# Reordering TensorE's work in the expert and feed-forward stage of a fused attention block

## The reference, cut to what matters

```python
x = x + attn(cond(x, ...))                     # x: 64 x 64 x 1024, float32
x = x + ffn(cond2(x, ...))

def cond2(x, ids, W, Wr, A, B):                # linear layer with gated LoRA experts
    base = einsum('btd,od->bto', x, W)
    logits = einsum('btd,ed->bte', x, Wr) + one_hot(ids) * 5.0
    topw, topi = top_k(logits, 2)
    gates = sum(one_hot(topi) * softmax(topw))
    h = einsum('btd,erd->bter', x, A)
    return base + 2.0 * einsum('bter,bte,eor->bto', h, gates, B)

def ffn(z):                                    # z in bfloat16, quantized to whole numbers per row
    qg, sg = dynamic_quant(z, inv_gate); qu, su = dynamic_quant(z, inv_up)
    inter = silu(quant_gemm(qg, sg, w_gate)) * quant_gemm(qu, su, w_up)
    qi, si = dynamic_quant(clip(inter, -10, 10), inv_inter)
    return quant_gemm(qi, si, w_down)
```

## Time and profile before

| what | value |
|---|---|
| time, median of 3 runs | 2393.21 us (2391.35 to 2397.13) |
| the profiled execution | 2398.05 us, its span 2396.1 us |
| TensorE busy | 2268.3 us (95% of the span) |
| TensorE weight loads busy | 1836.1 us (77%) |
| VectorE busy | 1307.3 us (55%) |
| ScalarE busy | 701.5 us (29%) |
| GpSimd busy | 1319.8 us (55%) |
| granted TensorE clock, mean | 0.982 |

### The profile page before, as it was taken

How to read it: one execution, slowest core, us unless ns; L and a number is a source line. 1 busy time by engine, 2 the same in 40 slices (tenths; PEclk the granted TensorE clock), 3 DMA queues, 4 the chain that set the end, 5 groups by cost and what they waited for, 6 DMA issues and landing times. The chain is left out here.

```text
span 2396.1 us, 48171 instructions
## 1 busy us (share of the span) xinstructions
PE 2268.3 (95%) x19520; PEld 1836.1 (77%) x19552; DVE 1307.3 (55%) x2248; ACT 701.5 (29%) x1122; POOL 1319.8 (55%) x1091
## 2 busy tenths in 40 slices
PE   6999999999999999999996999998999999999996
PEld 5888877888778888788885888886777777777774
DVE  5354464445644555545455322224677777777775
ACT  3222242222422223322223101012343333333332
POOL 6887878887778786888750000001455445445443
PEclk9999999999999999999998999998999999999998
DMA  4211122111221112121116844444011111111111
GB/s 139 65 60 57 61 98 68 63 59 63 80 89 56 66 54 72 65 69 54 63 37 202 239 165 132 132 166 132 19 53 53 39 49 53 47 41 53 53 35 44
DMA packets 130374, 188.33 MB, mean 79 GB/s; under 512 B 16162, under 2 KB 61346, under 8 KB 130210
## 3 DMA queue, kind: packets, MB, share of 16 engines
q1 hardware_dynamic: 118130, 165.92, 21.7%
q10 hardware_dynamic: 9216, 16.78, 1.8%
q0 software_dynamic: 2864, 3.28, 0.8%
HBM read 138.76 MB, written 50.33 MB: 79 GB/s over the span
## 5 line engine op out<-in xcount | busy, mean ns | idle before, releaser
L662 PE MATMUL acc<-y_hi,w_slot_hi 128*128 128x512 f32 x1344 | 541.6, 403 | 29.8 <-DVE unit L521 9.0
L662 PE MATMUL acc<-y_hi,w_slot_lo 128*128 128x512 f32 x1344 | 528.6, 393 | 0.0
L662 PE MATMUL acc<-y_lo,w_slot_hi 128*128 128x512 f32 x1344 | 527.7, 393 | 0.0
L313 POOL TENSOR_TENSOR w_slot_lo<-w_raw,w_slot_hi 128x512 fp32r<-128x512 f32 x329 | 424.3, 1290 | 26.3
L662 PEld LDWEIGHTS acc<-y_hi,w_slot_hi 128*128 128x128 f32 x1344 | 254.7, 189 | 90.2 <-issue 27.3
L311 POOL CAST w_slot_hi<-w_raw 128x512 fp32r<-128x512 f32 x329 | 218.0, 663 | 169.2 <-PE acc L662 134.8
L662 PEld LDWEIGHTS acc<-y_hi,w_slot_lo 128*128 128x128 f32 x1344 | 254.6, 189 | 54.8
L662 PEld LDWEIGHTS acc<-y_lo,w_slot_hi 128*128 128x128 f32 x1344 | 255.1, 190 | 48.9
L316 POOL TENSOR_TENSOR w_raw<-w_raw 128x512 f32<-128x512 f32 x188 | 259.4, 1380 | 25.6 <-DMA w_raw<-wu 20.5
L1094 POOL TENSOR_TENSOR raw<-raw,c_raw 128x1024 f32<-128x1024 f32 x32 | 76.2, 2380 | 347.0 <-DVE raw L1277 347.0
L1291 PE MATMUL z_ps<-w_hi,x_hi 128*128 128x512 f32 x512 | 219.1, 428 | 1.4 <-DVE w_lo L1150 1.2
(11 more groups left out here) (166 smaller groups left out, 3840.1 us busy)
## 6 DMA issues: line engine op xcount, KB each, us to landing
w_raw<-wu SPq DMA_DIRECT2D x192, 256.0 KB, 3.1
c_raw<-context_T SPq DMA_DIRECT2D x9, 2048.0 KB, 11.0
c_raw<-x_T SPq DMA_DIRECT2D x33, 512.0 KB, 4.6
x_c<-xT SPq DMA_DIRECT2D x64, 256.0 KB, 3.5
x_T<-out_c ACTq DMA_DIRECT2D x64, 256.0 KB, 3.7
out<-raw SPq DMA_DIRECT2D x32, 512.0 KB, 3.1
context_T<-cx SPq DMA_DIRECT2D x63, 256.0 KB, 3.5
x_raw<-x SPq DMA_DIRECT2D x27, 512.0 KB, 4.7
```

Source lines behind the costliest of these rows:

```text
L313: pool.tensor_tensor(w_lo[:, k], raw, w_hi[:, k].bitcast(F32), ALU.subtract).then_inc(w_set, 1)
L662: ins = pe.matmul(bank, w[:, k, c, :], v[:, k, c, :], start=(k in (0, 1, 5) and c == 0 and i == 0), stop=(c == C // 2 - 1 and i == 2), ski ...
```

## The change

In TensorE's body of this stage the order changes in four places. The transposes of the inner rows stand behind `linear` chunks 4 and 5, together with the scales' row; the down product stands behind `linear` chunks 6 and 7; the LoRA product follows it; gate and up stand last, one directly behind the other. In VectorE's body `zb` times inv_gate (`xg_set`) is ahead of `gt`. No instruction is added or removed, and the waits move with their instructions.

```diff
--- before.py
+++ after.py
@@ -1179,11 +1179,6 @@
 
         def body(t, j, has):
             two, three = (j + 2) % 4, (j + 1) % 4
-            if has(3):
-                dve.wait_ge(gu_mm, t * 2 - 5)
-                dve.wait_ge(p1_set, t - 3)
-                dve.scalar_tensor_tensor(gt[:], g_ps[:, 0], sc[:, three, 0:1], sg_all[:], ALU.mult, ALU.mult)\
-                    .then_inc(gt_set, 1)
             if has(2):
                 if isinstance(t, int) and t == 2:
                     dve.wait_ge(inv_in, 32)
@@ -1191,6 +1186,10 @@
                 dve.wait_ge(qb_set, t * 2 - 4)
                 dve.tensor_tensor(xs[0], zb[:], ig_all, ALU.mult).then_inc(xg_set, 1)
             if has(3):
+                dve.wait_ge(gu_mm, t * 2 - 5)
+                dve.wait_ge(p1_set, t - 3)
+                dve.scalar_tensor_tensor(gt[:], g_ps[:, 0], sc[:, three, 0:1], sg_all[:], ALU.mult, ALU.mult)\
+                    .then_inc(gt_set, 1)
                 dve.wait_ge(gu_mm, t * 2 - 4)
                 dve.wait_ge(p2_set, t - 3)
                 dve.scalar_tensor_tensor(ut[:], g_ps[:, 1], sc[:, three, 1:2], su_all[:], ALU.mult, ALU.mult)\
@@ -1325,21 +1324,23 @@
                 elif t > 1:
                     pe.wait_ge(hl_set, t - 1)
                 pe.transpose(ht_ps, hg[:], ident[:]).then_inc(ht_mm, 1)
+            if has(1):
+                linear(one, 1, range(4, 6), first)
             if has(3):
                 pe.wait_ge(ut_set, t - 2)
                 pe.wait_ge(qi_set, t - 2)
                 for c in range(CI):
                     ins = pe.transpose(qi_ps[:, c], qi[:, c * P:(c + 1) * P], ident_b[:])
                 ins.then_inc(ti_mm, 1)
-            if has(1):
-                linear(one, 1, range(4, 6), first)
-            if has(3):
                 pe.wait_ge(diag_set, t - 2)
                 if has(1):
                     pe.wait_ge(hl_set, t)
                 else:
                     pe.wait_ge(si_set, t - 3)
                 pe.matmul(si_ps, ones[:], diag[:], start=True, stop=True).then_inc(si_mm, 1)
+            if has(1):
+                linear(one, 1, range(6, 8), first)
+            if has(3):
                 if isinstance(t, int) and t == 3:
                     pe.wait_ge(dn_in, 16)
                 pe.wait_ge(qiT_set, t - 2)
@@ -1348,19 +1349,6 @@
                         ins = pe.matmul(g_ps[:, f // 4, (f % 4) * P:(f % 4 + 1) * P],
                                         dn_w[:, c, f * P:(f + 1) * P], qiT[:, c], start=(c == 0), stop=(c == CI - 1))
                 ins.then_inc(d_mm, 1)
-            if has(1):
-                linear(one, 1, range(6, 8), first)
-
-            def gate_up(i):
-                pe.wait_ge(qT_set, t * 2 - 3 + i)
-                for c in range(C):
-                    ins = pe.matmul(g_ps[:, i], qT[i][:, c], gu_w[:, c, i], start=(c == 0), stop=(c == C - 1))
-                ins.then_inc(gu_mm, 1)
-
-            if has(2):
-                if has(3):
-                    pe.wait_ge(o1_set, t - 2)
-                gate_up(0)
             if has(1):
                 if first:
                     pe.wait_ge(b_lo_set, 1)
@@ -1371,7 +1359,13 @@
                                         start=False, stop=(k == 2))
                     ins.then_inc(z_mm, 1)
             if has(2):
-                gate_up(1)
+                if has(3):
+                    pe.wait_ge(o1_set, t - 2)
+                for i in range(2):
+                    pe.wait_ge(qT_set, t * 2 - 3 + i)
+                    for c in range(C):
+                        ins = pe.matmul(g_ps[:, i], qT[i][:, c], gu_w[:, c, i], start=(c == 0), stop=(c == C - 1))
+                    ins.then_inc(gu_mm, 1)
 
         tile_loop(pe, body)
```

## The result

The changed kernel takes 2449.49 us (median of 4 runs, 2447.80 to 2453.02), the kernel before beside it 2394.64 us: the ratio is 1.0236, 95% interval [1.0215, 1.0257]. The forecast was slower, 2453 us. The profiled execution took 2449.45 us with a span of 2447.5 us; TensorE is busy for 2269.7 us, as before, which is now 93% of the span, and the granted clock is 0.982 of full speed, as before.

What follows compares the result with a forecast made beforehand. A loop through every engine and the load of x was taken as the bound: 1.11 + 1.0 = 2.1 us a tile, 58.8 us over 28 tiles, +1.1 for the first, total +59.9, giving 2453 us; range 2421 to 2464.

Steps and rivals of the forecast that it cites:

- The pace is set by the loop through the load of x: Expert and feed-forward stage: a 22.33 us loop through every engine and the load of x sets the pace, not TensorE's work.
- The down product behind one more piece: TensorE, last q transpose to end of down product: one more 1.48 us linear piece there, 23.44 against 22.33 us, +1.11.
- The meeting of zb x inv_gate with the last sum: VectorE's zb x inv_gate starts just ahead of GpSimd's sum with x (L1094) and holds it: +1.0 us a tile.
- The exchange at qi: TensorE: putting the qi transposes behind linear 4:6 removes the wait for qi, a gain of 0.38 us.
- The LoRA product: TensorE: LoRA product directly behind the down product takes over the cover, gate starts as now, so no gain or loss.
- L1081 pays back: GpSimd's L1081, 3.21 us, no longer meets zb x inv_gate and pays back to GpSimd's chain what L1094 lost.
- Edges: Outside the 28 tiles: +1.1 us for the first tile with a down product, 0 for the drain.
- C in the chances: Rival: a lower clock for TensorE from the added waits; chance 0.04.

Runs made afterwards that it cites:

- a3_free_load: Changed kernel with the load of x for the next tile freed from the current last sum and issued ahead of the store (wrong-row residual): 2416.44 us, ratio 1.0089.
- b3_free_load: Kernel before, with the load of x freed from the current last sum and issued ahead of the store (wrong-row residual): 2398.75 us, ratio 1.0013.
- a1_dve_back: Changed kernel with VectorE's old order (gt ahead of zb x inv_gate), TensorE's order as changed: 2421.19 us, ratio 1.0115 to the kernel before.
- b6_qi_later: Kernel before with only the transposes of qi moved behind linear 4:6, down product still directly behind the scales' row: 2400.11 us, ratio 1.0019.
- b7_lora_first: Kernel before with only the LoRA product ahead of gate, gate and up back to back, and VectorE's new order: 2382.78 us, ratio 0.9945.
- b1_dve_only: Kernel before with only VectorE's new order (zb x inv_gate, then gt): 2395.83 us, ratio 1.0004.
- a2_down_later: Kernel before with only the inner transposes behind linear 4:6 and the down product behind linear 6:8: 2431.06 us, ratio 1.0151.
- a4_aside: Changed kernel with ScalarE copying x aside, the next x loaded ahead of the store, and x_lo behind xi: 2407.23 us, ratio 1.0052 to the kernel before.

## Why the prediction was right

**The pace is set by the loop through the load of x.** Right for the changed kernel: TensorE waits 0.86 us at the logits for x and 1.43 us for qb, and freeing the load removes both (a3_free_load). For the kernel before it was only half of the matter. TensorE's last wait there is the one for qi, so the way over the q transposes, which I had followed, had 0.38 us to spare. The longer way from the same load shows in the tile of the earlier trace rows:

```profile
2032.87 2.41 POOL L1090 TENSOR_TENSOR x_lo<-c_raw,x_hi 128x1024 fp32r<-128x1024 f32 x1 [0.47 <-ACT x_hi L1123]
2032.90 2.92 DVE L1213 TENSOR_TENSOR xi<-ib,ii_all 128x512 f32<-128x512 bf16 x1
...
2038.82 0.61 ACT L1139 ACTIVATE qi<-xi 128x512 bf16<-128x512 f32 x1
```

x_hi releases x_lo at D + 11.98, x_lo holds xi, and qi is late. A way without the load is just as long, since freeing the load there gained nothing (b3_free_load); only with the load free and x_lo moved away did 22.21 come down to 21.31 us.

**The down product behind one more piece: +1.11 us a tile.** Measured by a1_dve_back: 23.15 - 22.21 = +0.94. The sign and the place are right. Of the 0.17 us missing, 0.08 is in the stretch from the q transposes to D, 6.65 instead of 6.73 us, because linear follows the transpose of hg after 0.03 us, not 0.12. The other 0.09 us isn't resolved; the tile that I took for the sum is at 22.33 us itself 0.12 us above the mean.

**The meeting of zb x inv_gate with the last sum: +1.0.** Measured +1.02 in the interval (a1_dve_back against the changed kernel), +0.92 in the length of L1094; L1187 led by 0.17 us, and I had said 0.05 to 0.16. That VectorE holds GpSimd when it starts first was priced from one meeting, that of L1213 with L1090 at 1788.93; it held for all 29 sums, with leads of 0.16 to 0.17 us. The same pair shows both directions: L1094 takes 3.30 us instead of 2.38 when VectorE is first (changed kernel), and L1192 takes 2.11 us instead of 1.22 when GpSimd is first (a1_dve_back). Which other pairs of instructions hold each other follows from neither; it has to be read from a trace for each pair.

**The exchange at qi: gain 0.38 us.** Right in the sum, wrong as a separate step: alone it costs (b6_qi_later, +0.14 us a tile), because linear 4:6 also covered ScalarE's copy of the transposes. Within the change the next piece, linear 6:8, takes over that cover.

**The LoRA product: no gain or loss.** This step was wrong by itself. Alone it gains 0.48 us a tile (b7_lora_first; VectorE's order, which is in it too, is worth nothing in b1_dve_only), mostly the same wait for qi that I had entered under the exchange. That the whole sum did not suffer is luck in part: the gain was counted once, under another name. In the changed kernel this step also brings zb to about D + 2.3 and so makes the meeting possible.

**L1081 pays back.** Right: 2.16 us instead of 3.21.

**Edges.** Instead of +1.1 for the first tile and 0 for the drain: from the logits of the body with the first down product to its D it takes 10.78 us instead of 10.24, +0.5; after the last of the 29 sums 60.5 us instead of 61.2, -0.7. The late landing in the first interval adds 1.0 us, and is within the 55.0 us; that it has to do with the change isn't shown.

**C in the chances, a lower clock for TensorE from the added waits.** That was an estimate of mine, and it didn't come: granted 1.00 of full speed from 1750 to 2350 us in the changed kernel, in spite of two waits in each tile, 2.3 us together. In the drain it is lower, 0.74 before and 0.80 and 0.78 after (2400 to 2420 and 2420 to 2440 us); from what wait on it would fall, no run shows.

In sum: 28 x 1.97 = 55.0 us against 28 x 2.1 = 58.8. The measured medians differ by 54.9 us.

## What to carry to other kernels

An engine that is busy 95% of the span may still not set the pace: follow one item through all queues and DMAs, and look at which stretch of the engine's order lies on that loop, because moving work into it costs its length, less the waits that it covers, though the engine does nothing more. Where an engine waits for several things in a row, the last wait tells which way is the longest: freeing the load gained nothing, because qi, which came last, had a second way as long (b3_free_load), and an earlier qi gained 0.48 us with the load as it was (b7_lora_first). So the parts of a change don't add: here +1.18 us a tile for both moves of a2_down_later, -0.48 us for the rest (b7_lora_first), and +1.97 us together. Before making an operand ready earlier on VectorE, look at what GpSimd runs at that moment, and let the one that is off the path start second: here that order was worth 1.02 us a tile (a1_dve_back).

## What was not expected of the hardware

The length of a VectorE instruction was no measure of how it suffered from GpSimd. gap, one column wide, took 2.07 us instead of 0.16 in a4_aside; ib, a tensor-scalar from SBUF to SBUF, 2.63 instead of 0.43 us in a3_free_load; and in the changed kernel L1217, another tensor-scalar, took 2.15 us instead of 0.49 (median 2.19 over 32), each beside x_lo (2.41 to 2.42 us) that had started first. In the changed kernel this happens to L1217 in 27 of 32 tiles (2.09 to 2.40 us) and costs nothing, since ScalarE is busy with qb until after it: in the tile above L1217 ends at 2085.62 and the second qb at 2087.15. A lead of 0.08 us was enough for x_lo over ib, and one of 0.37 us over gap.
